# Derived forms of h2 in three parts over a pair of steps, x split ahead in the first half, a shorter Newton step

## The reference

```python
h = _L0_tok_ref(...)   # dtA = A*dt; Cc = B*C*(exp(dtA) - 1)/A; h = 2*Re(einsum('chn,hnl->chl', Cc, exp(dtA*l)))
h = h + einsum('bsi,oi->bso', layernorm(h), attn_weight) + attn_bias
h2 = layernorm(h)
gates = softmax(einsum('bsi,ei->bse', h2, Wr))
lora = sum over e of 2.0 * gates[e] * (h2 @ A[e].T) @ Bm[e].T   # 4 experts of rank 8
h = h + (einsum('bsi,oi->bso', h2, W) + b) + lora
```

## Time and profile before

| | |
|---|---|
| median of 3 runs | 901.78 us (901.35 to 902.13) |
| profiled execution | 901.64 us, of it 899.7 us from first to last instruction |
| busy, share of the span | PE 765.4 us (85%), DVE 709.4 (79%), ACT 596.7 (66%), POOL 118.3 (13%) |
| granted PE clock, mean | 0.941 of full |
| chain that ended last, by engine | PE 43%, DVE 23%, ACT 9%, DMA 7%, SP's queue 7% |

### The profile page before, as it was taken

The page is one execution under the profiler, slowest core; times in us unless marked ns, Lnnn a source line. Parts: engine busy times, 40 slices in busy tenths (PEclk is TensorE's granted clock), DMA queues, the critical chain, the costliest instruction groups (busy, mean ns, idle before and its releaser), DMA issues.

```text
span 899.7 us, 15024 instructions
## 1 busy us (share of the span) xinstructions
PE 765.4 (85%) x5166; PEld 370.9 (41%) x5166; DVE 709.4 (79%) x1291; ACT 596.7 (66%) x979; POOL 118.3 (13%) x94
## 2 busy tenths in 40 slices
PE   2779999454989899898989899898989899898977
PEld 2624444222434344443434344343434344343433
DVE  7899996885987878787987878787987878787353
ACT  6778775665867677685777677685877677684120
POOL 2000202222020200202020200202020200202020
PEclk9979999886999999999989989899999999898999
DMA  8879676285243452526243452526243352526342
GB/s 295 247 143 172 148 160 130 72 186 101 51 93 82 83 111 50 123 50 141 54 95 77 82 111 50 122 50 140 55 91 81 82 111 50 117 50 129 51 93 62
DMA packets 258074, 94.21 MB, mean 105 GB/s; under 512 B 245424, under 2 KB 250416, under 8 KB 257912
## 3 DMA queue, kind: packets, MB, share of 16 engines
q1 hardware_dynamic: 257944, 93.66, 49.5%
q10 hardware_dynamic: 96, 0.13, 0.1%
HBM read 18.26 MB, written 16.78 MB: 39 GB/s over the span
## 4 chain that ended last, share of the span: by engine, by line
PE 43%; DVE 23%; ACT 9%; DMA 7%; issue 7%; SPq 7%; POOL 3%; DVEq 0%; POOLq 0%; ACTq 0%
PE ps_g L693 25%; PE ps_g L845 9%; PE ps_a L684 4%; DVE residual L1551 3%; DMA spare<-spare 3%; DVE u_split L1449 3%; SPq L524 2%; PE ps_x L845 2%; ACT junk L1047 2%; DVE form_tok L1879 2%; POOL form_sum L1400 2%; DVE residual L1886 2%; DMA forms<-form_tok 1%; SPq L511 1%; ACT form_tok L1230 1%
## 5 line engine op out<-in xcount | busy, mean ns | idle before, releaser
L693 PE MATMUL ps_g<-wa_hi,x 128*128 128x512 f16 x992 | 269.6, 388 | 7.3 <-DMA wa_lo<-residual 6.3
L693 PE MATMUL ps_g<-wa_lo,x 128*128 128x512 f16 x496 | 153.6, 389 | 0.0
L693 PEld LDWEIGHTS ps_g<-wa_hi,x 128*128 128x128 f16 x992 | 97.9, 100 | 130.5 <-issue 22.6
L684 PE MATMUL ps_a<-u_split,m_split 128*32 128x256 f16 x1344 | 58.1, 340 | 73.0 <-DVE u_split L1449 73.0
L845 PE MATMUL ps_g<-stage,forms 128*128 128x512 f16 x504 | 113.4, 379 | 7.1 <-DVE residual L1886 7.0
L1400 POOL TENSOR_TENSOR form_sum<-xn_b 128x512 f32<-128x512 f32 x14 | 18.1, 1290 | 581.0 <-DVE xn_b L1568 575.8
L684 PEld LDWEIGHTS ps_a<-u_split,m_split 128*32 128x32 f16 x1344 | 41.6, 117 | 92.2 <-issue 57.1
L845 PEld LDWEIGHTS ps_g<-stage,forms 128*128 128x128 f16 x504 | 48.5, 98 | 69.0 <-DVE residual L1886 9.3
L693 PEld LDWEIGHTS ps_g<-wa_lo,x 128*128 128x128 f16 x496 | 49.6, 100 | 61.8 <-issue 6.4
L1492 DVE TENSOR_TENSOR m<-x_t,q 128x512 f32<-128x512 f32 x32 | 22.0, 689 | 66.8 <-ACT x_t L1001 66.0
L1886 DVE SCALAR_TENSOR_TENSOR residual<-ps_g,unscale,residual 128x512 f32<-128x512 f32 x84 | 62.6, 745 | 14.7 <-PE ps_g L845 11.1
(11 more groups left out here) (273 smaller groups left out, 1450.2 us busy)
## 6 DMA issues: line engine op xcount, KB each, us to landing
out<-residual SPq DMA_DIRECT2D x124, 128.0 KB, 2.2
stage<-in_L_ffn_W SPq DMA_DIRECT2D x8, 512.0 KB, 14.0
x_raw<-in_x SPq DMA_DIRECT2D x38, 64.0 KB
residual<-in_L_attn_weight SPq DMA_DIRECT2D x4, 512.0 KB, 7.1
wf_hi<-in_x SPq DMA_DIRECT2D x1, 2048.0 KB, 9.4
xn_b<-in_L_ffn_W SPq DMA_DIRECT2D x4, 512.0 KB, 4.0
form_tok<-in_L_ffn_W SPq DMA_DIRECT2D x4, 512.0 KB, 5.4
forms<-form_tok SPq DMA_TRANSPOSE x106, 3.2
```

The lines of the kernel that those rows point to most:

```text
L684: mm = pe.matmul(ps_a[q * C:(q + 1) * C, a // 2, (a % 2) * WL:(a % 2 + 1) * WL], stationary[:, q, a * C:(a + 1) * C], moving[:, q, :], sta ...
L693: mm = pe.matmul(ps[:, o, :], x1_part(part, ps is ps_g2)[:, k, :], ws[:, k, o * HALF:(o + 1) * HALF], start=k == 0 and part == 0 and ws is ...
```

## The change

The forms S2, S4 and S3 of tile t-1 move from the end of step t-1 into the first half of step t, on ACT, DVE, POOL and SP. On DVE S2 and S4 come before `low_1(t,1)`, S3 after `low_u(t+1,0)`; at the end of the step only A22 and S1 stay, and behind `take_p7` and `low_u(t+1,1)`. S3 is now made in `form_sum`, where S1 was. POOL waits for `s4(t,1)` before S2 and S4 and for `attn(t,0)` before S3. ACT splits x(t+2) after `sines(t+1,1)`, SP transposes it after `turn_x1(t+1,0)`, and `join_x(t+2)` and `waves_ahead(t+2,0)` end the step; `phases(t+1,1)` moves up before `square_2(t,0)`. `newton` has three operations for four. In the start-up `turn_x(3)` comes before `turn_sums(1)`, `turn_x(4)` before `turn_sums(3)`, and `low_sums(3)` before `keep_h2(2,1)`. Not shown: `m_eps_sum`, a tenth small scale made once at the start.

```diff
--- before.py
+++ after.py
@@ -179,7 +179,7 @@
...
             return {A11: xn[:, 0:HALF], A12: xn[:, HALF:L], A22: xn_b[:, HALF:L], S1: form_sum[:, :],
-                    S2: xn_b[:, 0:HALF], S4: xn[:, HALF:L], S3: xn[:, 0:HALF]}[f]
+                    S2: xn_b[:, 0:HALF], S4: xn[:, HALF:L], S3: form_sum[:, :]}[f]
...
@@ -533,10 +533,12 @@
...
                 turn_form(t, S1, 3, 2)
+                turn_form(t, A22, 2, 7)
+
+            def turn_third_forms(t):
+
                 turn_form(t, S2, 4, 3)
                 turn_form(t, S4, 5, 5)
-                turn_form(t, S3, 6, 6)
-                turn_form(t, A22, 2, 7)
...
@@ -603,10 +605,10 @@
...
             turn_x2(1, 1)
+            turn_x(3)
             turn_sums(1)
...
-            turn_x(3)
             store(1, 0)
...
@@ -616,22 +618,25 @@
...
             turn_x1(3, 0)
+            turn_x(4)
             turn_sums(3)
...
-                if turns:
-                    turn_x(t + 1)
                 if stored:
...
                     load_x(t + 2)
+                turn_third_forms(t - 1)
                 turn_x1(t, 1)
                 turn_pair_lora(t - 1)
+                turn_form(t - 1, S3, 6, 6)
                 turn_first_forms(t)
...
                     turn_x1(t + 1, 0)
+                if loads:
+                    turn_x(t + 2)
                 store_pair(t - 1, 0, 1 - p)
...
@@ -640,6 +645,8 @@
...
             step(TILES - 1, 1, loads=False, turns=False)
+            turn_third_forms(TILES - 1)
+            turn_form(TILES - 1, S3, 6, 6)
             store_pair(TILES - 2, 1, 0)
...
@@ -1253,11 +1260,15 @@
...
                 rstd_guess(t, 1, stat_1, s_ssq1, s_log1, s_y1, m_eps)
+                if paired:
+                    high_form(t - 1, S2, 2)
+                    high_form(t - 1, S4, 3)
                 if waves:
...
                     sines(t + 1, 0)
+                    phases(t + 1, 1)
                 square_2(t, 0, p)
...
@@ -1266,9 +1277,11 @@
...
                     high_u(t + 1, 0)
+                if paired:
+                    high_form(t - 1, S3, 4)
                 high_first(t)
-            def second_half(t, p, waves=True, sums=False):
+            def second_half(t, p, waves=True, sums=False, x=True):
...
@@ -1276,42 +1289,38 @@
...
                     sines(t + 1, 1)
+                    if x:
+                        split_x(t + 2)
                 if sums:
...
                 rstd_guess(t, 1, stat_2, s_ssq2, s_log2, s_y2)
+                if waves:
+                    high_u(t + 1, 1)
                 high_form(t, A22, 0)
                 high_form(t, S1, 1)
-                high_form(t, S2, 2)
-                if waves:
-                    high_u(t + 1, 1)
-                high_form(t, S4, 3)
-                high_form(t, S3, 4)
+                if waves and x:
+                    join_x(t + 2)
+                    waves_ahead(t + 2, 0)
...
             step(1, 1, True)
+            split_x(3)
             high_sums(1)
-            split_x(3)
             waves_ahead(3, 0)
...
             high_sums(2)
-            waves_ahead(3, 1)
+            decays(3, 1)
             second_half(2, 0, sums=True)
-            split_x(4)
-            waves_ahead(4, 0)
-            join_x(4)
...
                 first_half(t, p)
-                waves_ahead(t + 1, 1)
+                decays(t + 1, 1)
                 second_half(t, p)
-                split_x(t + 2)
-                waves_ahead(t + 2, 0)
-                join_x(t + 2)
...
@@ -1389,27 +1401,40 @@
...
-            def add_forms(t):
+            def add_first_form(t):
...
                 else:
-                    pool.wait_ge(s_form_lo, LOWERED * tau + 1)
+                    pool.wait_ge(s_form_lo, LOWERED * tau)
                 pool.tensor_tensor(form_sum[:, :], xn_b[:, 0:HALF], xn_b[:, HALF:L], ALU.add).then_inc(s_form, 1)
+
+            def add_other_forms(t, beside=True):
+
+                tau = t - FIRST
+                if beside:
+                    pool.wait_ge(s_s4, 2 * t + 4)
                 pool.wait_ge(s_form, 4 * tau + 1)
...
                 pool.tensor_tensor(xn[:, HALF:L], xn[:, HALF:L], xn_b[:, 0:HALF], ALU.subtract).then_inc(s_form, 1)
-                pool.tensor_tensor(xn[:, 0:HALF], xn_b[:, HALF:L], xn_b[:, 0:HALF], ALU.subtract).then_inc(s_form, 1)
+                if beside:
+                    pool.wait_ge(s_g1, 2 * t + 3)
+                pool.wait_ge(s_form_lo, LOWERED * tau + 3)
+                pool.tensor_tensor(form_sum[:, :], xn_b[:, HALF:L], xn_b[:, 0:HALF], ALU.subtract).then_inc(s_form, 1)
...
                 sum_weights(j)
-            add_forms(FIRST)
-            with pool.Fori(FIRST + 1, TILES) as t:
-                add_forms(t)
+            add_first_form(FIRST)
+            add_other_forms(FIRST)
+            with pool.Fori(FIRST + 1, TILES - 1) as t:
+                add_first_form(t)
+                add_other_forms(t)
+            add_first_form(TILES - 1)
+            add_other_forms(TILES - 1, beside=False)
...
@@ -1510,24 +1537,23 @@
...
-            def newton(J, stat, guess, step_done, added=EPS):
+            def newton(J, stat, guess, step_done, added=L * EPS):
                 dve.wait_ge(guess, J + 1)
-                dve.tensor_scalar(stat[:, 5:6], stat[:, 2:3], 1 / L, added, ALU.mult, ALU.add).then_inc(step_done, 1)
-                dve.wait_ge(step_done, 4 * J + 1)
-                dve.tensor_scalar(stat[:, 6:7], stat[:, 4:5], stat[:, 4:5], stat[:, 5:6], ALU.mult, ALU.mult)\
+                dve.tensor_scalar(stat[:, 5:6], stat[:, 2:3], added, stat[:, 4:5], ALU.add, ALU.mult)\
                     .then_inc(step_done, 1)
-                dve.wait_ge(step_done, 4 * J + 2)
-                dve.tensor_scalar(stat[:, 6:7], stat[:, 6:7], -0.5 * XSCALE, 1.5 * XSCALE, ALU.mult, ALU.add)\
+                dve.wait_ge(step_done, 3 * J + 1)
+                dve.tensor_scalar(stat[:, 6:7], stat[:, 5:6], stat[:, 4:5], -0.5 * XSCALE / L, ALU.mult, ALU.mult)\
                     .then_inc(step_done, 1)
-                dve.wait_ge(step_done, 4 * J + 3)
-                dve.tensor_scalar(stat[:, 7:8], stat[:, 6:7], stat[:, 4:5], None, ALU.mult).then_inc(step_done, 1)
-                dve.wait_ge(step_done, 4 * J + 4)
+                dve.wait_ge(step_done, 3 * J + 2)
+                dve.tensor_scalar(stat[:, 7:8], stat[:, 6:7], 1.5 * XSCALE, stat[:, 4:5], ALU.add, ALU.mult)\
+                    .then_inc(step_done, 1)
+                dve.wait_ge(step_done, 3 * J + 3)
...
                 J = 2 * T + i
-                newton(J, stat_1, s_y1, s_nw1, m_eps)
+                newton(J, stat_1, s_y1, s_nw1, m_eps_sum)
                 if by_act(T, i):
...
@@ -1561,7 +1587,7 @@
...
                 else:
-                    dve.wait_ge(s_form_lo, LOWERED * (t - FIRST))
+                    dve.wait_ge(s_form_lo, LOWERED * (t - FIRST) - 1 + i)
                 if isinstance(t, int) and t == FIRST and i:
...
@@ -1979,19 +2005,19 @@
...
+                keep_h(t, 1)
                 if ended:
-                    keep_h(t, 1)
                     end_22(t - 2, p)
-                    if following:
-                        make_m(t + 1, 0)
-                    normalise_1(t, 1)
-                    if following:
-                        round_turns(t + 1, 0)
-                    low_1(t, 1)
-                    if following:
-                        low_m(t + 1, 0)
-                else:
-                    next_h(t, 1, t, 0, following)
+                if following:
+                    make_m(t + 1, 0)
+                normalise_1(t, 1)
+                if following:
+                    round_turns(t + 1, 0)
+                low_form(t - 1, S2, 4)
+                low_form(t - 1, S4, 5)
+                low_1(t, 1)
+                if following:
+                    low_m(t + 1, 0)
                 keep_h2(t, 0, p)
...
@@ -2001,8 +2027,9 @@
...
                     low_u(t + 1, 0)
+                low_form(t - 1, S3, 6)
+                take_p5(t - 1, 1 - p)
                 low_first(t)
-                take_p5(t - 1, 1 - p)
                 take_p6(t - 1, 1 - p)
...
@@ -2012,14 +2039,11 @@
...
                 end_12(t - 1, 1 - p)
+                take_p7(t - 1, 1 - p)
+                if following:
+                    low_u(t + 1, 1)
                 low_form(t, A22, 2)
                 low_form(t, S1, 3)
-                take_p7(t - 1, 1 - p)
-                low_form(t, S2, 4)
-                if following:
-                    low_u(t + 1, 1)
-                low_form(t, S4, 5)
-                low_form(t, S3, 6)
                 end_21(t - 1, 1 - p)
...
@@ -2040,16 +2064,13 @@
...
             next_h(3, 0, 2, 1, True)
+            low_sums(3)
             keep_h2(2, 1, 0)
             make_u(3, 1)
-            low_sums(3)
             normalise_2(2, 1, 0)
+            low_u(3, 1)
             low_form(2, A22, 2)
             low_form(2, S1, 3)
-            low_form(2, S2, 4)
-            low_u(3, 1)
```

(22 more changed lines are left out.)

## The result

The kernel after takes 794.87 us (793.99 to 795.24, 4 runs), beside 901.57 (900.99 to 902.13, 4 runs) for the kernel before on the same chip: a ratio of 0.8815, 95% interval 0.880 to 0.883. Its profiled execution has a span of 792.2 us at a mean granted clock of 0.982. The forecast was 799, range 788 to 828.

The account below looks back on a forecast made before the run. PE was taken to bound the kernel, idling for low u and then running at half clock, 50.70 us per period against a floor of 43.62. 901.64 - 82.8 (loop) - 14.0 (start-up) - 5.6 (end) = 799.2; forecast 799, range 788 to 828.

Parts of the forecast that it names:

- The three parts: Savings forecast by place: start-up to s4(3,1) 14.0 us, loop of twelve periods 80.2, from s4(15,1) to the end 8.2.
- every cover: Loop slack before PE's due times: 0.8 and 1.0 us in the first half, 0.8 and 0.7 in the second; none broken.
- floor: Loop: what PE needs per period at full clock, 43.62 us, against a period of 50.70 before.
- The jitter: Loop: would break a cover now and then, so the period was taken as 43.8 us beside 43.62.
- POOL's hold: First half: POOL's S4 slows make_m's first product on DVE by between 0 and 1.06 us; 1.06 taken.
- the estimate of 4.2 per step: Loop: DVE time lost if all four POOL operations each held a two-SBUF-input DVE instruction, 4 x 1.06; about 815 us in all.
- Moving the phases: First half, ACT: phases now stand ahead of square_2(t,0), take 2.06 us and put 1.6 us on the path.
- Rival (a): Loop: a cover fails, product 6 or s4 waits 1 to 2.5 us each period at full clock; 811 to 829; chance 0.22.
- Rival (b): Loop: low_u comes late, PE still stands 2.5 to 4 us and drops its clock; 841 to 878; chance 0.10.
- Rival (c): Whole kernel slower: chip grants less clock under unbroken work, decisive below 0.83 of full clock; 928 us at 0.80; chance 0.03.
- The term of x(3): Start-up: x(3) transposed earlier removes DVE's idling; 9 us taken, between 5 and 11.1.
- the 4.2 counted: End: product 2 of the last tile no longer waits for end_21 behind all five forms; 4.2 us saved.

Follow-up runs that it names:

- e8: Kernel after plus an unused DVE instruction over 5 x 1024 elements per step between product 7's take and low u(t+1,1): 884.07 us, ratio 0.9807.
- e12: Kernel after plus an unused DVE instruction of about 2.2 us ahead of product 1's take in each step: 807.50 us, ratio 0.8958.
- e5: Kernel after with low A22 and S1 put back ahead of product 7's take and low u(t+1,1): 812.35 us, ratio 0.9010.
- e3: Kernel before with u(t+1,1) ahead of all five forms and x(t+2) split, turned and joined earlier: 863.69 us, ratio 0.9563.
- e11: Kernel after with phases of (t+1,1) put back behind the high halves of the first forms on ACT: 795.09 us, ratio 0.8813.
- e6: Kernel after plus an unused DVE instruction over 1024 elements per step between product 7's take and low u(t+1,1): 800.66 us, ratio 0.8881.
- e7: Kernel after plus an unused DVE instruction over 3 x 1024 elements per step between product 7's take and low u(t+1,1): 844.64 us, ratio 0.9372.
- e9: Kernel after with x alone put back in the loop: transposed at the head of SP's step, split and joined at ACT's end: 842.87 us, ratio 0.9352.
- e4: Kernel after with keep_h2(2,1), make_u(3,1), low_u(3,1) and high_u(3,1) moved ahead of the last weight sums in the start-up: 794.70 us, ratio 0.8805.
- e1: Kernel before with only low_u(t+1,1) and high_u(t+1,1) moved ahead of all five forms: 930.38 us, ratio 1.0308.

## Why the prediction was right

The two spans differ by 107.5 us for 102.4 forecast. The three parts miss in the same direction, by 2.6, 2.1 and 0.4, and the mechanism is the one laid out: every cover held.

**The floor and the loop.** The period is 43.71 for a floor of 43.62 summed from pieces. The jitter that was to break a cover now and then (12 x 0.1) didn't show, and the first period's low clock cost 1.51 (45.22 - 43.71) where the text had 2.57: together the 2.1 us. That the mean of 43.83 agrees with the 43.8 taken is in part luck, since the 43.8 was for jitter and the 0.12 above 43.71 is that low clock. 2.57 itself was well sized for the loop before (2.79 in e8, behind a stop as long); the price differs with the place and the stop, 1.3 to 3.0 in these runs.

**First half.** The take of product 1 was laid out to end at 20.0 and ends at 19.5; product 6 at 20.7 for 20.8. The cover is 1.2 by the rows and 1.1 by e12, not 0.8. The mis-sized term is POOL's hold: taken as 1.06, measured 1.19 - 0.68 = 0.51, since POOL's operations last 1.28 here, not 1.60, and only the end of the second meets `make_m`. Its mechanism is right: the one instruction held is the SBUF-fed one under S4, and `keep_h` beside S2 keeps 1.28. So the estimate of 4.2 per step from the Trainium skill's rule (SBUF, State Buffer, "Who interferes with whom") falls, not by the rule but by how few such instructions POOL meets: neither A22's nor S1's low half (0.68 each) runs beside it any more. In e5, where A22 does, it takes 1.29. Where POOL makes all its forms beside such work, in e3, they cost DVE 3.3 us per step; their new places took that hold away. Moving the phases was costed at 1.6 on this chain; e11 shows 1.3, and 0 of the time.

**Second half.** Low u's end was forecast at 42.9 in the step and comes at 547.5 - 504.6 = 42.9; cover 0.7 forecast, 0.6 by e6, 0.8 by the rows. Rival (a), 811 to 829, needed a cover to fail by 1 to 2.5 us at full clock: e5, with stops of 1.28, gives 812, e12 with 0.9 gives 808. Its upper end is priced too low: stops of about 2.5 brought the low clock too in e7 (845) and mostly in e9 (843). Rival (b), 841 to 878, is e7 at its lower end; e8 (884) lies above it, since its stop of 4.70 is longer than the 2.5 to 4 that (b) has.

**Clock under unbroken work.** Rival (c) is refuted by the loop's row: 524.38 us without a gap at a mean of 1.00.

**Start-up.** 16.6 instead of 14.0, 0.6 beyond the upper bound of 16. The term of x(3) was 9 and measures 10.1:

```profile
151.09 0.69 DVE L1519 TENSOR_TENSOR m<-x_t,q 128x512 f32<-128x512 f32 x1 [2.67 <-ACT x_t L1008]
...
190.36 0.75 DVE L1876 SCALAR_TENSOR_TENSOR forms<-xn_b,scale,forms 128x512 f16<-128x512 f32 x1 [0.24 <-ACT forms L1208]
```

(161.23 in the earlier trace rows); the last sums are low at 191.1, not 193.7, so another 1.4 is gained between the two, whose cause stays open. From there to s4(3,1) it is 6.0, as laid out. e4 shows that the wait of 16.09 is not worth its size: 9.4 us less of it came back as other waits and low clock.

**End.** The stretch sheds 8.6 us for 8.2. Product 2 of the last tile waits 0.90 instead of 4.21 and runs at full clock (0.38 for one matmul, 0.59 there). PE's timeline of the kernel before, then of the kernel after:

```profile
868.06 0.39 PE L852 MATMUL ps_g<-lb,lora_t_pair 98*128 98x512 f16 x1 [1.11 <-DVE residual L1886]
...
766.48 0.38 PE L852 MATMUL ps_g<-wf_hi,forms 128*128 128x512 f16 x1 [0.90 <-DVE residual L1912]
```

That is 3.3 of the 4.2 counted. The wait just ahead of it in the kernel before, 1.11 us of a lora matmul for a take, is gone as well, and the prediction doesn't name it. By the granted clock of the kernel before, 0.50 from 872.66 to 875.1 and from 822.02 to 826.8, the low clock cost there about 1.4 and 2.8 us, for 1.4 and 2.6 taken. 3.3 + 1.1 + 1.4 + 2.8 = 8.6.

**What the prediction missed** without paying for it: it never named `last_lora`'s wait for the take of product 7. e1 and e3 show it, 1.9 and 2.3 us, there in the shadow of a later wait; the change hasn't got it, because it moves u behind that take and the forms behind both. A forecast of e3 from the same layout missed by 28 us; by the rows of e3, DVE had 3.3 us of POOL's hold and a wait of 1.57 for ACT that it didn't count.

## What to carry to other kernels

In a pipeline with one critical engine, lay out one period of every other engine against that engine at its floor. That gave the worth of the whole set of edits (108 us here), and none of one edit alone (-6 us, +28 us, and -39 for the two). A wait of the critical engine costs time only where it ends last: in e3 PE stood 2.3 us in each step and lost clock in half of them, and the period was the same, because product 6 would have waited for DVE anyway. List for each instruction moved all that wait behind it, and what the other engines do beside it in its new place. Measure a cover by putting in idle work of known length: e6 and e12 gave 0.6 and 1.1 us.
